# A four-batch decoder layer on one core: the order of the opening and of the last batch's feed-forward

## What is computed

```python
x = LN(x + causal_self_attention(x))               # Wq, Wk, Wv, Wo with biases
x = LN(x + cross_attention(x, ctx of 64 rows))     # masked keys, no biases
g = silu(bitlinear(x, w_gate)); u = bitlinear(x, w_up)   # 256 -> 1024
x = LN(x + bitlinear(g * u, w_down))                # 1024 -> 256
```

## Time and profile before

| | |
|---|---|
| median of 3 runs (lowest, highest) | 849.23 us (847.72, 849.62) |
| the profiled execution | 847.58 us, of it 845.5 us span |
| PE busy | 797.8 us (94%) |
| DVE busy | 687.9 us (81%) |
| ACT busy | 574.6 us (68%) |
| POOL busy | 342.9 us (41%) |
| mean granted TensorE clock | 0.996 |

### The profile page before, as it was taken

The page is one execution under the profiler, slowest core; times in us unless marked ns, Lnnn a source line. Parts: engine busy times, 40 slices in busy tenths (PEclk is TensorE's granted clock), DMA queues, the critical chain, the costliest instruction groups (busy, mean ns, idle before and its releaser), DMA issues.

```text
span 845.5 us, 20914 instructions
## 1 busy us (share of the span) xinstructions
PE 797.8 (94%) x7816; PEld 395.7 (47%) x7816; DVE 687.9 (81%) x1261; ACT 574.6 (68%) x751; POOL 342.9 (41%) x582
## 2 busy tenths in 40 slices
PE   8889999999999989999999999999999999999997
PEld 6534345344564434534454344543545443445645
DVE  4899998948998699887999689974899848836698
ACT  1277856467965588655885679866597579864595
POOL 3832454344333055431544245442425403552344
PEclk9999999999999999999999999999999999999999
DMA  7422102100211011100131020101110001010001
GB/s 233 94 83 58 46 20 72 42 21 3 49 47 58 1 41 38 26 26 10 40 87 26 11 79 2 39 11 29 39 52 2 8 1 52 2 51 1 2 2 52
DMA packets 37189, 32.90 MB, mean 39 GB/s; under 512 B 9828, under 2 KB 33252, under 8 KB 37092
## 3 DMA queue, kind: packets, MB, share of 16 engines
q1 hardware_dynamic: 33844, 28.93, 12.2%
q0 software_dynamic: 1536, 1.58, 0.8%
q10 hardware_dynamic: 1712, 1.05, 0.5%
HBM read 14.55 MB, written 4.19 MB: 22 GB/s over the span
## 4 chain that ended last, share of the span: by engine, by line
PE 64%; DVE 20%; ACT 6%; issue 5%; POOL 2%; ACTq 1%; DMA 0%; SPq 0%; POOLq 0%; DVEq 0%
PE ps L1031 12%; DVE shift L1376 11%; PE ps L826 8%; PE ps L1016 7%; PE ps L994 6%; PE ps L839 5%; PE ps L965 3%; PE ps L790 3%; PE ps L977 3%; PE ps L892 3%; PE ps L922 2%; PE ps L917 2%; PE ps L815 2%; PE ps L934 2%; ACT probs L1137 2%
## 5 line engine op out<-in xcount | busy, mean ns | idle before, releaser
L1376 DVE TENSOR_REDUCE shift<-ps 128x2 f32<-128x1024 f32 (+2 forms) x320 | 343.9, 1111 | 39.6 <-PE ps L994 19.4
L1137 ACT ACTIVATE probs<-ps 128x1024 f32<-128x1024 f32 (+3 forms) x384 | 294.2, 811 | 103.9 <-PE ps L1016 101.4
L1031 PE MATMUL ps<-probs,v_aug 128*32 128x512 f32 (+3 forms) x1536 | 157.5, 499 | 0.1
L705 POOL TENSOR_SCALAR_AFFINE_SELECT probs<-probs 128x512 f32<-128x512 f32 x128 | 80.7, 640 | 163.8 <-ACT probs L1137 163.0
L994 PE MATMUL ps<-k_stack,q_stack 48*128 48x512 f16 (+3 forms) x768 | 114.6, 330 | 13.2 <-DVE shift L1376 4.8
L1016 PE MATMUL ps<-q_stack,k_stack 49*128 49x512 f16 (+3 forms) x768 | 116.0, 328 | 10.4 <-DVE shift L1376 4.9
L1016 PEld LDWEIGHTS ps<-q_stack,k_stack 49*128 49x128 f16 x768 | 37.6, 93 | 112.9 <-ACT probs L1137 37.9
L994 PEld LDWEIGHTS ps<-k_stack,q_stack 48*128 48x128 f16 x768 | 40.3, 93 | 97.2 <-DVE shift L1376 34.5
L1000 PE MATMUL ps<-causal,pick_h 64*128 64x64 bf16 x1024 | 53.3, 190 | 0.0
L1078 ACT ACTIVATE full<-ps,bias_scaled,kq_scale 128x512 f32<-128x512 f32 x32 | 25.0, 780 | 41.5 <-PE ps L839 32.3
L1000 PEld LDWEIGHTS ps<-causal,pick_h 64*128 64x128 bf16 x1024 | 46.4, 96 | 14.4 <-issue 0.5
(11 more groups left out here) (205 smaller groups left out, 1361.0 us busy)
## 6 DMA issues: line engine op xcount, KB each, us to landing
q_stack<-part_sb SPq DMA_DIRECT2D x168, 32.0 KB, 2.0
k_stack<-part_sb SPq DMA_DIRECT2D x144, 32.0 KB, 2.0
xT<-in_x_cols SPq DMA_DIRECT2D x8, 512.0 KB, 4.5
xt<-in_x SPq DMA_DIRECT2D x8, 512.0 KB, 4.1
out_x<-xt SPq DMA_DIRECT2D x7, 512.0 KB, 3.5
q_stack<-shiftT SPq DMA_DIRECT2D x128, 1.0 KB
k_stack<-part_sb POOLq DMA_DIRECT2D x48, 32.0 KB, 2.0
region<-in_w_gate SPq DMA_DIRECT2D x4, 256.0 KB, 4.2
```

Of the source, the lines that this page charges most:

```text
L705: pool.affine_select(out=blk, in_=blk, compare_op=ALU.is_ge, fill=0.0, base=0, pattern=[[0, HG], [1, P]], channel_multiplier=-1).then_inc( ...
L1031: mm = pe.matmul(ps[DV * i:DV * (i + 1), SUM_BANK, off:BANK], v_aug[:, kb, at:at + DV], probs_of(b, n)[:, i, :], start=first, stop=last)
L1137: act.activation(probs_of(b, n)[:, 2 * p:2 * p + 2, :], pair(u)[:, :, 0:BANK - off], ACT.Exp, scale=exp_scale).then_inc(probs_ready, 1)
L1376: dve.tensor_reduce(to[:, :, pairs[0]:pairs[-1] + 1, qb % TH], pair(u)[:, :, 0:len(pairs) * w].rearrange("p j (h w) -> p j h w", w=w), AX. ...
```

## The change

1. DVE no longer waits for `consts_ready` at its start. `tops` of the first batch takes each operand as it lands: Wk, first half of x, Wq, second half of x, then the biases. The wait for `consts_ready` moves into `take_bound`.
2. PE runs 36 transposes of the identity in place of 70, then the first half (`d = 0`) of the first four projections, into four banks, and only then waits for `consts_ready` and `tops_ready`. The units `kq` add the second halves.
3. ACT runs one activation of one column as soon as its input is set.
4. The last batch's `post(b, 0)` becomes a chain `h` with a room of its own, `early_room`, in the stack copy that even batches use; four areas of `late_room` go to `probs`. `k2` of a later batch waits for the last cross-attention copy of the batch before it.
5. `ORDER` is new as a whole, with 59 stirs in place of 70.

```diff
-STIRS = 70
+STIRS = 59
+WARM_UP = 36
...
-    "ffrr6r0sr6sz0ffr0r6wr0ssffgr6m01m23ggm45r6gm23m01m45r6m01r2m45m01m23r6m01m45a23a01aw6a23z4w4a01m23aa56om01m4"
+    "rr6r0sr1sgr2sr3sr6r1wr0ggfgm23m01m45r6m01m23m45r6m01m23r4m01fffm56m23m01a45a23w6aa01w4a23am56m01om23m45w6ssa"
...
-        chains["p"] += (context(b) if b else []) + post(b, 0)
+        chains["p" if b < NB - 1 else "h"] += (context(b) if b else []) + post(b, 0)
...
+            if at >= 32:
+                v = probs[:, (at - 32) * BANK:(at - 32 + n) * BANK]
+                return v.bitcast(dt) if dt != F32 else v
...
+        early_room = room(within, within(8, 2).rearrange("p (d q) -> p d q", d=CC),
+                          (10, 2), (12, 4), (16, 2), (20, 1), (8, 8), (18, 2), (21, 2))
         late_room = room(within, within(24, 2).rearrange("p (d q) -> p d q", d=CC),
-                         (26, 2), (0, 8), (28, 4), (22, 1), (8, 8), (20, 2), (16, 4))
+                         (26, 2), (0, 8), (28, 4), (40, 1), (32, 8), (41, 2), (43, 4))
+
+        def room_at(b, r):
+
+            return late_room if is_late(b, r) else early_room if b == NB - 1 else main_room
...
+            begun = [n for n in range(SLOTS) if not find["kq", 0, n].before]
+
+            def project(u, ds):
+
+                t, e, h = pieces[u.idx]
+                if u.b == 0:
+                    pe.wait_ge(kq_loaded[1 - t], 16)
+                pe.wait_ge(x_loaded[h], 16 * (u.b + 1))
+                for d in ds:
+                    mm = pe.matmul(ps[:, u.bank, :], (wk, wq)[t][:, d, e * P:(e + 1) * P],
+                                   xT[:, h, d, :], start=(d == 0), stop=(d == CC - 1))
+                return mm
...
+                    mm = project(u, [d for d in range(CC) if b > 0 or d > 0 or u.idx not in begun])
                 elif kind == "bound":
                     if b == 0:
-                        stir(u, 70)
+                        stir(u, WARM_UP)
+                        for n in begun:
+                            project(find["kq", 0, n], [0])
+                        pe.wait_ge(consts_ready, 1)
                     pe.wait_ge(tops_ready, b + 1)
...
                 elif kind == "k2":
+                    if b > 0:
+
+                        pe.wait_ge(act_taken, find["pv2", b - 1, (NG - 2, 1)].taken)
...
+            act.wait_ge(pool_ready, 5)
+            act.activation(first_out[:], round_c[:], ACT.Identity, bias=round_c[:, 0:1])
...
                 for h in range(QC):
+                    if b == 0:
+                        dve.wait_ge(kq_loaded[1 - h], 16)
+                        link(dve.tensor_reduce(w_top[:, :, h], (wk, wq)[h][:], AX.X, ALU.max, apply_absolute_value=True))
                     dve.wait_ge(x_loaded[h], 16 * (b + 1))
                     link(dve.tensor_reduce(x_top[:, h, :], xT[:, h, :, :], AX.X, ALU.max, apply_absolute_value=True))
                 link(dve.tensor_tensor(x_top[:, QC, :], x_top[:, 0, :], x_top[:, 1, :], ALU.max))
+                for t, bias in enumerate((bk_c, bq_c)) if b == 0 else ():
+                    dve.wait_ge(bias_loaded[1 - t], 16)
+                    link(dve.tensor_reduce(b_sum[:, t:t + 1], bias[:], AX.X, ALU.add, apply_absolute_value=True))
...
+                if b == 0:
+                    dve.wait_ge(consts_ready, 1)
...
-            dve.wait_ge(consts_ready, 1)
-            for t, bias in enumerate((bk_c, bq_c)):
-                dve.wait_ge(bias_loaded[1 - t], 16)
-                link(dve.tensor_reduce(b_sum[:, t:t + 1], bias[:], AX.X, ALU.add, apply_absolute_value=True))
-            for t, w in enumerate((wk, wq)):
-                dve.wait_ge(kq_loaded[1 - t], 16)
-                link(dve.tensor_reduce(w_top[:, :, t], w[:], AX.X, ALU.max, apply_absolute_value=True))
```

94 lines of the change are left out of this document (44 added, 50 removed).

## The result

| | before | changed |
|---|---|---|
| median of 6 runs each, us | 849.42 (847.7 to 852.86) | 839.38 (838.2 to 842.74) |
| profiled execution: time / span, us | 847.58 / 845.5 | 839.25 / 837.2 |
| its mean granted clock | 0.996 | 0.992 |
| ratio of the medians | | 0.9881 [0.9853, 0.9909] |

The changed kernel is 10.0 us faster.

What follows compares the result with a forecast made beforehand. The prediction took PE to bound the kernel, DVE between 40 and 60 us, and a chain of single steps in the opening. Its terms, 3.5 + 1.3 + 0.4 = 5.2 us, gave 844.0 from 849.23, range 840.0 to 848.3.

Steps and rivals of the forecast that it cites:

- Operands as they land: Opening, on DVE: taking weights and x at landing ends the product at 10.9 instead of 14.45, 3.5 us earlier.
- The first activation: Opening, on ACT: a tiny activation at about 3 us hides the table load, 1.28 us less.
- Begun projections: Opening, on PE: four first halves, about 0.45 us each, end at about 10, ahead of the product at 10.9.
- The six DMAs of a piece and their landing are unchanged: SP's first moves: 7.4 us to the first maximum, taken as unchanged, which puts that maximum at 24.0.
- The DVE-bound stage: From 24 to 55 us: DVE has the same work, nothing gained or lost by more than a row.
- the feed-forward loads: Weight loads moved later on SP: 0 to 1 us of ACT, which has slack; taken as 0.
- the bulk: Attention's start to last maximum: new order but same units and 44 stirs; 0, with 3 us either way.
- the slower rival: ACT's back-to-back weight sums and a late third matrix stall PE; time 851.5; chance 0.07.
- The tail: Last batch's end: the moved product with V brings the norm about 0.9 us forward; taken as 0.4 us gained.
- The term of 0.37: Tail: PE's idle time in front of `x1T`, 0.37 us, is what the earlier norm can return.
- Against the profiled execution, 847.58 ... the median stands 1.65 higher: Baseline: the 5.2 us gain gives 842.4 against the profile and 844.0 against the median of 849.23.
- The clock rival: Gap before the first maximum: five idle PE us drop TensorE's clock, losing 1.7 us, hence 845.7; chance 0.2.

Runs made afterwards that it cites:

- no_table: The changed kernel without the early small activation on ACT; 842.16 us, ratio 0.9911 to the kernel before.
- no_rooms: The changed kernel with the last batch's parts in the old rooms, order unchanged; 838.62 us, ratio 0.9868 to the kernel before.

## Why the prediction was right or wrong

**Operands as they land: right.** 3.5 us forecast; the bound moved from 14.51 to 11.05, 3.46.

**The first activation: right.** 1.3 forecast, 1.29 in `no_table`. The first copy stood at 13.14 for 13.05.

**Begun projections: mis-sized, and without a term of their own.** The prediction let four first halves run ahead of the bound at "about 0.45 us each". The trace has them 0.86 us apart:

```profile
7.11 1.02 PE L850 MATMUL ps<-xT,w_k 128*128 128x512 f32 x2
...
9.68 1.02 PE L850 MATMUL ps<-xT,w_q 128*128 128x512 f32 x2
```

That is 3.4 us of PE's work moved into its idle time, and not 1.8. The prediction put the saved transposes at nothing, which no run contradicts, and the relief of the third and fourth copy at nothing; it did not ask what the begun halves themselves are worth. Without them 5.8 us are lost, about 1.8 through the clock and 4.0 with the clock held, as the copies wait and PE has 3.4 us more to do before its first score product. The 3.5 us from the first copy to SP's first move were copied from before (17.91 to 21.40) and held because the projections were begun. So the sum up to SP's first move came out right (16.6 for 16.66), and the total did not suffer; advice on what to keep would have.

**"The six DMAs of a piece and their landing are unchanged": wrong, the step that cost most inside the trace.** 7.4 taken, 5.51 measured, a gain of 1.9 us, all of it in the landing of the sixth move: 4.00 us before and 2.10 now, while the issue of the sixth stands 3.3 us behind that of the first in both. It lies within the bounds of 2.3 either way that were kept, but the value taken was the middle. Two causes are shown with sizes, the loads ahead (0.57) and ACT's moves beside (0.35). What makes up the other 1.0 is open; `no_table` shows only that the same moves land later when all of it runs 2.1 us later.

**The DVE-bound stage, the feed-forward loads, the bulk: right.** The lead was 6.7 us at the first score product and 6.7 at the last maximum; in between it lay from 4.9 to 7.2 at nine maxima of ten, and 1.4 were lost by 56 us, where the clock stretch is. ACT summed `w_gate` and `w_up` back to back, as the slower rival had it, at 50.95 and 53.04, and `w_down` at 69.06 without waiting for a load:

```profile
67.05 2.11 ACT L1161 ACTIVATE probs<-ps 128x1024 f32<-128x1024 f32 x2
69.06 1.90 ACT L1202 ACTIVATE turned<-xt 128x2048 bf16<-128x2048 f32 x1
```

PE's longest wait of the kind that had most was 0.7 us between 55 and 735, so the slower rival had no place.

**The tail: right in its place, undersized.** 0.4 forecast. The two plain traces show 1.0, and 1.6 with the stores. The term of 0.37, PE's idle time in front of `x1T`, was read as the most that the earlier norm could return; but the lead grew by 0.6 us up to that norm and by 0.4 more by the last ones. The rooms were worth nothing, as said: `no_rooms` has 838.62.

**"Against the profiled execution, 847.58 ... the median stands 1.65 higher": wrong, the other failed step.** It added the same gain to both. The 847.58 was one of the best executions of the kernel before, with a clock of 0.996, where most had 0.990, and the median stands 1.84 above it; the changed kernel's profiled run stands 0.13 under its own median. The clock differs from run to run, and the typical run of the changed kernel has the higher one. About 1.7 of the 10.0 us are in the medians and not in the two spans.

So: 3.5 + 1.3 as forecast, 1.9 more for the landing, 1.0 for the tail in place of 0.4, 0.6 at the store, make the span's 8.3, and 1.7 lie between the spans and the medians.

**The clock rival: right that a thin stretch would bring the lower level, and spared by chance in its place.** It expected five idle us ahead of the first score product. PE was idle for 1.61, since its four second halves took 0.86 us each and not 0.45, which ended its projections at 20.56 and not 19, and since the moves landed sooner. In this trace the clock held there and fell at 35.5, in the stage that DVE bounds; behind the same wait in `no_rooms` it fell. The prediction took 1.7 us for such a fall, and the two traces of before give about 1.2 for 3.4 us of it.

The Trainium skill, "TensorE: Matmul & The Clock Gate", section "HAM oscillation", ties the fall to waits on transfers. The variants show falls at such waits, of 1.60 to 3.33 us. The traces also show falls without them, and the dip of rows 8, which the prediction took to agree with the page, is one: ahead of 54.9 PE waited 0.40 us for ACT, then 0.66 and 0.79 for DVE. Its last wait:

```profile
54.30 0.39 PE L994 MATMUL ps<-k_stack,q_stack 48*128 48x512 f16 x2 [0.79 <-DVE shift L1376]
```

In the changed kernel, from 32.5 to 35.5, PE's waits were 0.2 to 0.8 us each, none on a transfer. The last and longest:

```profile
35.52 0.61 PE L1040 MATMUL ps<-q_stack,k_stack 49*128 49x512 f16 x2 [0.79 <-DVE shift L1410]
```

## What to carry to other kernels

When a chain of copies feeds the first transfer, price the last copy of the piece and not the first, and count how much of an engine's work leaves the path when it is done early in idle time: here 3.4 us, and without it the median was 4.0 higher with the clock held. Before adding a forecast gain to a baseline, look at the granted clock of several runs of it; 5 us of spread in 850 here went with stretches at half clock, and seven four-matmul stirs in the thin places of TensorE went with a median 1.8 us lower. Before reading a variant's trace for its gain, look where its run stands among the others: two traces here were of the fastest and the slowest run of their variant. A landing time of small moves is a term of its own: it was 2.1 us in one order and 4.0 in another.

## What the runs showed of the hardware

- The granted clock fell to 0.50 without PE standing idle for long: PE's longest wait ahead of the fall at 35.5 was 0.79 us. Around three falls PE was busy 0.73, 0.72 and 0.88 us in a window of 2 of the view. The stretches lasted about 3.4, 6.8 or 10.2 us in the traces, and each 3.4 us cost 1.2 us or so, by one pair of traces.
- The same kernel got them in different places and numbers in two traces (6.8 us in all in one of before, 20.4 in the other), and its runs' times follow their mean clock: 846.6 to 847.2 us at 0.996, 851.2 to 852.3 at 0.988.
- The same wait does not always bring a fall: behind 1.57 to 1.61 us ahead of the first score product the clock fell within 1.3 us in one trace (`no_rooms`) and held for more than 10 us in three. The kernel before has both as well: held behind 2.62, and a fall 1.6 us behind a wait of 2.59.
- At the lower level a projection of four 128x512 f32 matmuls took 3.19 and 3.41 us, at the full clock 1.88.
- The clock's rise at the start was not at one moment: the last of the 36 transposes started at 6.99 in the changed kernel's trace and between 7.4 and 8.4 in its variants, and the bound moved between 10.98 and 11.93 with it.
- ACT's table load at its first use cost 1.28 us and nothing visible behind it.
- Small moves from one place of SBUF to another, six in a row, landed 2.1 us after the issue of the last in the changed kernel and 3.8 to 4.0 in both traces of before.
